# Moving the second mixture's late weight pieces from the first mixture's tile loop to the attention's sampling chunks, in halves by ACT and DVE

## The chip, the cores and the metric

The kernel runs on one core of a Trainium2 chip. The metric is the device time of one execution in microseconds (us); lower is better. Engines are called PE (TensorE), DVE (VectorE), ACT (ScalarE), POOL (GpSimd) and SP (SyncE, which here only issues DMAs).

## The reference, cut to what matters

```python
h = tok_ref(x, weight, bias)                        # 32 sequences of 166 tokens, width 128
h = h + recurrence(layernorm(h))                    # complex linear recurrence, 256 states
h = h + first_mixture(layernorm(h), gate, w1, w2)   # 16 experts of 512, top 2
h = h + sparse_attention(layernorm(h), Wq, Wk, Wv, Wo, idx_sample)
h = h + second_mixture(layernorm(h), w1, b1, w2, b2, router_w, router_b)   # 64 experts of 256, top 42

# first_mixture: sums of silu over an expert's tokens come first, w2 afterwards
h_sum = einsum('tef,te->ef', silu(einsum('td,efd->tef', x, w1)), mask)
y_mean = einsum('ef,edf->ed', h_sum / counts, w2)
out = einsum('tk,tkd->td', routing_w, y_mean[top_idx])

# sparse_attention: every query is scored against 38 sampled keys, the 25 best queries of a head attend in full
QK_sample = einsum('bhld,bhsd->bhls', Q, K[:, :, idx_sample]) * scale
M = QK_sample.max(-1) - QK_sample.mean(-1)
```

## The kernel before

The program is a chain of stages, each a block with one hand-written instruction stream for each engine, tied by semaphores. Every stream is executed in order: a wait at its head holds all that stands behind it. Stages end with a barrier of all engines.

**The expert weights of the second mixture** come in fp32 (8 MB for each of two matrices) and are needed as pairs of fp16 numbers: a rounded value and a correction. They are cut into 32 pieces of 128x1024. Pieces 0 to 15 belong to `ExpertWeights` (L2143) and are split by POOL in four instructions (a cast, a subtraction, a scaling, an addition; `pool_pieces`, L2195). Pieces 16 to 31 belong to `LateWeights` (L2215), which does the same beside the first mixture (`pool_piece`, L2260). The results of all but the first group of experts are stored to DRAM (`expert_factors`) and loaded back by the second mixture.

**The first mixture** (`FirstMixture`, L1273) works on 43 tiles of 384 token slots (`NST`), each of one expert. For each tile SP fetches the slots from DRAM with a transposing DMA into a ring of 8 (L1346). PE forms the 512 hidden features in two sets of 256 (L1403; a set is 4 matmuls of 384 columns into two banks; 4 sets fit), ACT applies silu to a set in place (L1368), DVE sums each feature over the 384 slots (L1374), and then the set is free for PE. So there are 86 sets. SP's stream of this loop (`sync`, L1329) also holds the loads and stores of the late pieces and the four 1 MB loads of the matrix `w2` (`sync_down`, L1325), placed between the transposes by `W2_AT`, `KEEP_FROM` and `KEEP_EVERY`.

**The attention's first stage** (`sparse_attention`, L1502) takes the norm's statistics (its first part), and then works through 16 chunks of two sequences (the sampling part). In chunk `c` PE's stream is, by `work(c, j)`:

```python
samples(c, j, 0); samples(c, j, 1)        # needs ACT's copies kx of chunk c, all four
query(c + 1, 1 - j); key(c + 1, 1 - j)
norm.pe_spread(pe, c + 2, j)              # needs POOL's diagonal of chunk c + 2
for q in range(4):
    token_major(c + 1, 1 - j, q)          # from q = 2 on needs ACT's copy of q - 2
    sampled_scores(c, j, q)
```

PE thus works on the scores of chunk `c` and on the projections of chunk `c + 1` in one pass. ACT's `work(c + 1)` (query and key copies, then three copies for each of four q, L1632 to L1643) goes on at that time, while DVE's `work(c)` takes the maxima of the scores of chunk `c` (L1711, L1713), and before q = 3 normalises chunk `c + 2` (L1269, L1691). ACT is therefore one chunk ahead of DVE. Two banks hold token-major products (4 and 5), and two the scores.

POOL's stream is: diagonals 0 and 1, a piece, diagonal 2, a piece, and so on (L1603 to L1607), so diagonal `c + 2` stands behind the piece that follows diagonal `c + 1`. Before, three pieces are done ahead of diagonal 0. `ExpertWeights` has two raw buffers; SP loads piece `n + 1` before it stores piece `n` (`sync_pieces`, L2185). At the end POOL makes tables for the attention proper (L1608 to L1622).

## Time and profile before

| | |
|---|---|
| median of 3 runs | 2063.67 us (2062.18 to 2066.14) |
| the profiled execution: its own time | 2067.39 us |
| the profiled execution: its span, first to last instruction | 2065.7 us |
| busy: PE, PEld, DVE, ACT, POOL | 1870.1, 1349.7, 1676.4, 1378.0, 1455.0 us |
| granted TensorE clock, mean | 0.939 of full speed |
| first mixture's tile loop | 283.3 to 397.8 us |
| rest of the first mixture | 397.8 to 428.9 us |
| attention: statistics | 428.9 to 455.0 us |
| attention: sampling chunks | 465.9 to 583.2 us |
| attention proper, then the second mixture's set-up | 583.9 to 826 us |
| second mixture, 64 experts | 826 us to the end |

PE is a TensorE matmul, PEld its weight load. "Busy" is the time in which an engine executes; idle time is put down to the instruction that ended it (the releaser). A "granted clock" of 1.00 is 2.4 GHz, one of 0.50 is 1.2 GHz. The rows of the trace stand in a section of their own below.

### The profile page before, as it was taken

The page shows a single profiled execution, that of the slowest core. Times are in us where ns is not written, and L with a number is a line of the kernel's source. Part 1 is how long each engine was busy: PE and PEld are TensorE (multiplying, and loading weights), DVE is VectorE, ACT ScalarE, POOL GpSimd, SP SyncE. Part 2 cuts the span into 40 slices and gives each one's busy share as a digit, 9 for nine tenths or more (in the row PEclk, how much of TensorE's full clock was granted, in tenths as well). Part 3 has the DMA queues.
Part 4 walks back from the last instruction along what each step waited for, and adds up shares of the span by engine and source line. Part 5 has one row for each costly group of instructions (what it writes and reads, how often), then busy time and mean ns, then how long its engine had stood idle before and what let it go on. Part 6 is the DMA issues. An engine that isn't in the chain of part 4 may idle for free.

```text
span 2065.7 us, 50535 instructions
## 1 busy us (share of the span) xinstructions
PE 1870.1 (91%) x17038; PEld 1349.7 (65%) x17038; DVE 1676.4 (81%) x4833; ACT 1378.0 (67%) x2149; POOL 1455.0 (70%) x1098
## 2 busy tenths in 40 slices
PE   7887436789989978999999999999999999999998
PEld 5555213456669855777777777777777777777776
DVE  5887736555678788899999999999999999999998
ACT  4134525424435545888888888888888888888886
POOL 2216679559800032888888888888888888888887
PEclk9998768789989965999999999999999999999999
DMA  3011289523200010000000200000100000000000
GB/s 93 21 35 63 81 246 257 124 67 94 90 1 1 22 63 1 2 2 0 0 0 3 82 2 0 0 0 35 49 1 0 0 0 2 2 10 11 10 11 19
DMA packets 64334, 77.56 MB, mean 38 GB/s; under 512 B 38932, under 2 KB 47028, under 8 KB 62132
## 3 DMA queue, kind: packets, MB, share of 16 engines
q1 hardware_dynamic: 61364, 70.08, 11.7%
q0 software_dynamic: 2816, 5.45, 0.8%
q8 instruction: 94, 1.54, 0.3%
q14 instruction: 60, 0.49, 0.1%
HBM read 42.97 MB, written 24.08 MB: 32 GB/s over the span
## 4 chain that ended last, share of the span: by engine, by line
PE 58%; DVE 3%; issue 2%; ACT 1%; POOL 0%; ACTq 0%; DVEq 0%; POOLq 0%
PE bank L2679 30%; PE bank L2662 28%; DVE m_work L2553 1%; DVE m_best L2550 1%; DVE m_work L2544 0%; PE bank L2632 0%; DVE m_ut L1269 0%; ACT m_h L2485 0%; DVE m_best L2543 0%; DVE m_ex L2555 0%; DVE h L2591 0%; DVE m_red L2556 0%; DVE m_row L2536 0%; POOL m_diag L1255 0%; ACT m_hidden L2482 0%
## 5 line engine op out<-in xcount | busy, mean ns | idle before, releaser
L2679 PEld LDWEIGHTS bank<-weights,m_h 128*128 128x128 f16 x10752 | 649.6, 98 | 194.4 <-DVE hc L2582 82.6
L2430 POOL TENSOR_TENSOR m_h<-m_hidden,m_h 128x896 f16<-128x896 f32 x384 | 725.9, 1890 | 32.0
L2679 PE MATMUL bank<-weights,m_h 128*128 128x128 f16 x10752 | 724.6, 219 | 10.7 <-POOL m_h L2430 2.1
L2582 DVE SCALAR_TENSOR_TENSOR hc<-bank,m_shares,hc 128x128 f32<-128x128 f32 x2688 | 727.2, 342 | 4.3 <-PE bank L2679 4.3
L2482 ACT ACTIVATE m_hidden<-bank,m_b 128x896 f32<-128x896 f32 x384 | 386.9, 1007 | 197.6 <-PE bank L2662 197.5
L2567 DVE TENSOR_TENSOR m_h<-bank,m_h 128x896 f16<-128x896 f32 x384 | 419.2, 1092 | 116.8 <-ACT m_h L2485 116.7
L2428 POOL TENSOR_SCALAR m_h<-m_hidden 128x896 f16<-128x896 f32 x384 | 360.8, 939 | 117.9 <-ACT m_hidden L2482 99.5
L2662 PE MATMUL bank<-m_u_first,weights 128*128 128x448 f16 (+1 forms) x1536 | 417.8, 354 | 5.5 <-DVE h L2591 5.5
L2662 PE MATMUL bank<-m_u_second,weights 128*128 128x448 f16 (+1 forms) x1536 | 417.7, 354 | 0.0
L2479 ACT ACTIVATE bank<-bank,m_b 128x896 f32<-128x896 f32 x384 | 377.6, 983 | 0.6 <-PE bank L2662 0.6
L2485 ACT ACTIVATE m_h<-bank 128x896 f16<-128x896 f32 x384 | 349.1, 909 | 0.0
L2662 PEld LDWEIGHTS bank<-m_u_second,weights 128*128 128x128 f16 x1536 | 150.8, 98 | 141.4 <-issue 2.0
L699 POOL DMA_INDIRECT expert_slots<-weights,ro_slot x88 | 88.9, 1010 | 76.5 <-DVE weights L839 50.6
L1403 PE MATMUL bank<-lru_ut,weights 128*128 128x384 f16 x344 | 74.1, 373 | 74.5 <-DMA lru_ut<-expert_slots 60.0
L1374 DVE TENSOR_REDUCE lru_xc<-bank 128x2 f32<-128x768 f32 x86 | 77.2, 950 | 67.4 <-ACT bank L1368 67.3
L2662 PEld LDWEIGHTS bank<-m_u_first,weights 128*128 128x128 f16 x1536 | 118.2, 98 | 8.1 <-DVE h L2591 6.4
L1368 ACT ACTIVATE bank<-bank 128x768 f32<-128x768 f32 x86 | 64.7, 798 | 82.6 <-PE bank L1403 82.1
L2399 POOL MEMSET m_row<- 128x96 f32 x1 | 0.2, 178 | 157.0 <-POOLq L1827 157.0
L1403 PEld LDWEIGHTS bank<-lru_ut,weights 128*128 x344 | 37.3, 108 | 110.7 <-issue 99.9
L980 POOL TENSOR_TENSOR lru_diag<-ident,rstd 128x332 f32<-128x332 f32 x16 | 13.5, 858 | 65.3 <-PE bank L1147 41.3
L1711 DVE TENSOR_REDUCE at_peak<-bank 83x8 f32<-83x304 f32 x64 | 30.0, 468 | 35.4 <-PE bank L1769 35.2
L1751 PE MATMUL bank<-at_w_qk,at_ut 128*83 128x384 f32 x128 | 52.9, 501 | 0.0
(359 smaller groups left out, 2153.9 us busy)
## 6 DMA issues: line engine op xcount, KB each, us to landing
weights<-expert_factors SPq DMA_DIRECT2D x12, 1024.0 KB, 8.8
lru_w_in<-e_w_dram SPq DMA_DIRECT2D x16, 512.0 KB, 4.5
expert_factors<-lru_w_out SPq DMA_DIRECT2D x16, 512.0 KB, 4.3
ew_raw<-e_w_dram SPq DMA_DIRECT2D x16, 512.0 KB, 3.9
weights<-w_dram SPq DMA_DIRECT2D x16, 256.0 KB, 2.8
weights<-w_dram SPq DMA_DIRECT2D x4, 1024.0 KB, 6.6
expert_factors<-ew_made SPq DMA_DIRECT2D x8, 512.0 KB, 3.0
xs<-x_dram SPq DMA_DIRECT2D x4, 996.0 KB, 11.8
```

The source lines that it names most:

```text
L699: g.indirect_dma_start(out=self.k.slots, out_offset=bass.IndirectOffsetOnAxis(ap=self.slot[0:size, q, n:n + 1], axis=0), in_=self.u_tok[0: ...
L1374: v.tensor_reduce(self.part[:, j // PARTS, j % PARTS * FP:(j % PARTS + 1) * FP], self.set_banks(j), X, ALU.add).then_inc(self.summed, 1)
L1403: last = t.matmul(self.set_banks(n)[:, f % FP], self.w0_parts[m][:, bass.ds(expert * FF0 + f * 128, 128)], self.xt[:, j % RING, m], start= ...
L2428: g.tensor_scalar(h1[:, x, 0], hidden[:, x], 1.0 - SHARE, 1.0, ALU.mult, ALU.mult).then_inc(first_of[1], 1)
L2430: g.tensor_tensor(h1[:, x, 1], hidden[:, x], h1[:, x, 0], ALU.subtract).then_inc(second_of[1], 1)
L2479: sc.activation(banks0(x), banks0(x), ACT.Gelu, bias=b1[:, bass.ds(grp * GE + e, 1), 0]).then_inc(gelu[0], 1)
L2482: sc.activation(two(hidden[:, x % 2]), banks1, ACT.Gelu, bias=b1[:, bass.ds(grp * GE + e, 1), 1]).then_inc(gelu[1], 1)
L2485: sc.activation(two(h0[:, x, 0]), banks0(x), ACT.Copy, scale=1.0 - SHARE).then_inc(first_of[0], 1)
L2567: v.tensor_tensor(two(h0[:, x, 1]), banks0(it), two(h0[:, x, 0]), ALU.subtract).then_inc(second_of[0], 1)
L2582: last = v.scalar_tensor_tensor(acc[:, m * TW:(m + 1) * TW], y[q][:, (n - start) * TW:(n - start + 1) * TW], shares[:, m, e:e + 1], acc[:, ...
L2662: last = t.matmul(bank[:, q], k.weights[:, grp % 2, m, at], uu[:, bass.ds(tb * WB + q * HW, HW)], start=(m == 0), stop=(m == 1))
L2679: last = t.matmul(y[q][:, (n - start) * TW:(n - start + 1) * TW], factors[:, m, n * TW:(n + 1) * TW], k.weights[:, grp % 2, 2 + m, at], st ...
```

## The change

- The late pieces 16 to 31 leave the first mixture. They are cut in halves (128x512, 32 of them), and two halves go with each sampling chunk: ACT rounds a half to fp16 and writes a scaled fp32 copy of it to a buffer `wide`, of which there is one; DVE makes the correction of both in one instruction. ACT's part stands behind q = 1 and q = 3 of its `work(c)`, DVE's behind q = 1 and q = 3 of its own. SP loads and stores the halves.
- The pieces 0 to 15 of POOL are all done beside the sampling chunks; none ahead of diagonal 0. SP's stream for both kinds is one loop over `n`, with the load of piece `n + 1` at the end of round `n`.
- The first mixture's `w2` (4 MB) is loaded into four separate places before the slots' blank ends are written, ahead of the tile loop. The tile loop's SP stream has transposes alone.
- Of the 86 sets, every sixth (14, those with j % 6 == 5) is summed by ACT, with the accumulator output of its silu, in two instructions of 384 columns; DVE sums the other 72.
- The squares of the attention's statistics share memory with the halves' buffers, so SP waits for the last square before it loads a half.

```diff
@@ recurrence, SP
+            mixture.sync_second(sp, y_ready)
             routing.sync_fill(sp)
-            mixture.sync(sp, y_ready)
+            mixture.sync(sp)
@@ FirstMixture
+    def sync_second(self, sp, outputs_made):
         sp.wait_ge(outputs_made, NC)
-        late.sync_load(sp, 0)
-        late.sync_load(sp, 1)
-        sp.wait_ge(k.w0_split, NC)
-        self.sync_down(sp, 0)
+        sp.wait_ge(self.k.w0_split, NC)
+        for q in range(4):
+            self.sync_down(sp, q)
...
-            if j in self.W2_AT:
-                self.sync_down(sp, 1 + self.W2_AT.index(j))
-            if j >= self.KEEP_FROM and (j - self.KEEP_FROM) % self.KEEP_EVERY in (0, 2):
-                late.sync_keep(sp)
...
     def act(self, act):
         for j in range(self.PARTS * NST):
             act.wait_ge(self.up, j + 1)
-            self.nc.scalar.activation(self.set_banks(j), self.set_banks(j), ACT.Silu).then_inc(self.silu, 1)
+            if self.act_sums(j):
+                for f in range(self.FP):
+                    at = j % self.PARTS * self.FP + f
+                    last = self.nc.scalar.activation(self.set_banks(j)[:, f], self.set_banks(j)[:, f], ACT.Silu,
+                                                     accum_out=self.part[:, j // self.PARTS, at:at + 1])
+            else:
+                last = self.nc.scalar.activation(self.set_banks(j), self.set_banks(j), ACT.Silu)
+            last.then_inc(self.silu, 1)
@@ sparse_attention, SP
-                k.expert_weights.sync_pieces(sp, *PIECES_N3)
-                k.expert_weights.sync_pieces(sp, *PIECES_SAMPLE)
+                k.expert_weights.sync_load(sp, 0)
+                k.expert_weights.sync_load(sp, 1)
+                sp.wait_ge(stats.var, NC + DEEP)
+                k.late_weights.sync_load(sp, 0)
+                k.late_weights.sync_load(sp, 1)
+                for n in range(2 * GROUP):
+                    for s in range(2):
+                        k.late_weights.sync_load(sp, 2 * n + 2 + s)
+                        k.late_weights.sync_keep(sp, 2 * n + s)
+                    if n:
+                        k.expert_weights.sync_keep(sp, n - 1)
+                    if 1 <= n < 2 * GROUP - 1:
+                        k.expert_weights.sync_load(sp, n + 1)
@@ sparse_attention, POOL
-                k.expert_weights.pool_pieces(pool, *PIECES_N3)
-                first, end = PIECES_SAMPLE
                 for c in range(NC):
                     norm.pool_diagonal(pool, c, c % 2, stats)
-                    if 1 <= c <= end - first:
-                        k.expert_weights.pool_pieces(pool, first + c - 1, first + c)
+                    if c:
+                        k.expert_weights.pool_pieces(pool, c - 1, c)
+                k.expert_weights.pool_pieces(pool, NC - 1, NC)
@@ sparse_attention, ACT and DVE, behind q = 1 and q = 3
+                        if q % 2:
+                            k.late_weights.act_piece(act, c, q // 2)
...
+                        if q % 2:
+                            k.late_weights.dve_piece(dve, c, q // 2)
@@ LateWeights
     def sync_load(self, sp, i):
         if i >= 2:
             sp.wait_ge(self.raw_read, i - 1)
...
+    def sync_keep(self, sp, i):
         sp.wait_ge(self.split, i + 1)
...
+    def act_piece(self, act, c, s):
+        follows = not isinstance(c, int) or c
+        act.wait_ge(self.raw_in[s], 16 * c + 16)
+        if follows:
+            act.wait_ge(self.kept_out[s], 16 * c)
+        self.nc.scalar.activation(self.made[:, s, 0], self.raw[:, s], ACT.Copy).then_inc(self.rounded, 1)
+        if s or follows:
+            act.wait_ge(self.split, 2 * c + s)
+        self.nc.scalar.activation(self.wide, self.raw[:, s], ACT.Copy, scale=1.0 / SHARE).then_inc(self.raw_read, 1)
+
+    def dve_piece(self, dve, c, s):
+        dve.wait_ge(self.rounded, 2 * c + s + 1)
+        dve.wait_ge(self.raw_read, 2 * c + s + 1)
+        self.nc.vector.scalar_tensor_tensor(self.made[:, s, 1], self.made[:, s, 0], 1.0 - 1.0 / SHARE, self.wide, ALU.mult,
+                                            ALU.add).then_inc(self.split, 1)
```

How the streams stand now is shown at two places. The first is ACT's stream in the sampling part, from q = 1 of a chunk to the next chunk's copies (at_qt and hc are the query and key copies, at_kx the last of the three copies of a q, lw_room the halves' buffers). Before:

```order
L1643 ACTIVATE at_kx<-bank 83x128
L1643 ACTIVATE weights<-bank 83x128 [waits at_token_major_ready]
L1643 ACTIVATE at_v_all<-bank 83x128
L1643 ACTIVATE at_kx<-bank 83x128
L1633 ACTIVATE at_qt<-bank 128x332 [waits at_qt_ready]
L1635 ACTIVATE hc<-bank 128x332 [waits at_kt_ready]
L1643 ACTIVATE weights<-bank 83x128 [waits at_token_major_ready]
```

and with the change:

```order
L1668 ACTIVATE at_kx<-bank 83x128
L2292 ACTIVATE lw_room<-lw_room 128x512 [waits lw_raw_in1]
L2295 ACTIVATE lw_room<-lw_room 128x512 [waits lw_split]
L1658 ACTIVATE at_qt<-bank 128x332 [waits at_qt_ready]
L1660 ACTIVATE hc<-bank 128x332 [waits at_kt_ready]
L1668 ACTIVATE weights<-bank 83x128 [waits at_token_major_ready]
```

Between a chunk's last copy and the next chunk's query copy stand now two instructions, of which the second waits for DVE (`lw_split`).

The second place is SP's stream in the sampling part. Before, loads (L2176) and stores (L2183) of POOL's pieces alternate:

```order
L2176 DMA ew_raw<-e_w_dram 128x1024 x2
L2176 DMA ew_raw<-e_w_dram 128x1024 [waits ew_raw_read] x8
L2183 DMA expert_factors<-ew_made 128x2x1024 [waits ew_split]
L2176 DMA ew_raw<-e_w_dram 128x1024 [waits ew_raw_read]
L2183 DMA expert_factors<-ew_made 128x2x1024 [waits ew_split]
```

With the change (L2210 is the load of a piece of POOL, L2274 and L2281 the load and store of a half; the rows begin with the first two loads):

```order
L2210 DMA ew_raw<-e_w_dram 128x1024 x2
L2274 DMA lw_room<-e_w_dram 128x512 [waits n3_variance]
L2274 DMA lw_room<-e_w_dram 128x512
L2274 DMA lw_room<-e_w_dram 128x512 [waits lw_raw_read]
L2281 DMA expert_factors<-lw_room 128x2x512 [waits lw_split]
L2274 DMA lw_room<-e_w_dram 128x512 [waits lw_raw_read]
L2281 DMA expert_factors<-lw_room 128x2x512 [waits lw_split]
L2274 DMA lw_room<-e_w_dram 128x512 [waits lw_raw_read]
L2281 DMA expert_factors<-lw_room 128x2x512 [waits lw_split]
L2274 DMA lw_room<-e_w_dram 128x512 [waits lw_raw_read]
L2281 DMA expert_factors<-lw_room 128x2x512 [waits lw_split]
L2210 DMA ew_raw<-e_w_dram 128x1024 [waits ew_raw_read]
```

The third load of a POOL piece, piece 2, now stands behind the stores of the halves 0 to 3, and each later one behind two more.

## Rows read from the trace of the kernel before

**Rows 1.** Stretches: us, PE PEld DVE ACT POOL busy, PEclk, DMA share, GB/s.
```profile
283.00:398.00 115.00, 74.30 (x346) 37.51 (x347) 77.16 (x86) 64.69 (x86) 95.96 (x61) 0.84 0.96 237
456.00:466.00 10.00, 10.00 (x26) 5.61 (x26) 5.80 (x10) 2.88 (x12) 9.67 (x8) 0.55 0.18 53
466.00:583.00 117.00, 113.53 (x471) 70.21 (x469) 70.20 (x208) 50.55 (x215) 90.76 (x69) 1.00 0.25 81
744.00:812.00 68.00, 51.03 (x174) 37.45 (x175) 65.53 (x394) 36.47 (x132) 23.79 (x28) 0.50 0.00 1
```

**Rows 2.** Groups by line, the tile loop, 280 to 398 us.
```profile
L1374 DVE TENSOR_REDUCE lru_xc<-bank 128x2 f32<-128x768 f32 x86 | 77.2, 950 | 67.4 <-ACT bank L1368 67.3
L1403 PE MATMUL bank<-lru_ut,weights 128*128 128x384 f16 x344 | 74.1, 373 | 74.5 <-DMA lru_ut<-expert_slots 60.0 <-issue 9.9 <-DVE lru_xc L1374 3.3
L1368 ACT ACTIVATE bank<-bank 128x768 f32<-128x768 f32 x86 | 64.7, 798 | 82.6 <-PE bank L1403 82.1
```

**Rows 3.** SP's queue in order of time, the tile loop's first transposes.
```profile
280.20 5.36 SPq L1346 DMA_TRANSPOSE lru_ut<-expert_slots  x4
```

**Rows 4.** Groups by line, the recurrence stage, 60 to 285 us.
```profile
L1092 DVE SCALAR_TENSOR_TENSOR weights<-weights 128x512 f16<-128x512 f16 x16 | 11.4, 714 | 1.6 <-ACT weights L1008 1.6
L1008 ACT ACTIVATE weights<-weights 128x512 f32<-128x512 f32 x16 | 9.9, 616 | 5.9 <-DVE weights L1092 5.9
L764 ACT ACTIVATION_READ_ACCUMULATOR weights<-weights 128x1 f32 x44 | 8.5, 193 | 0.0
L794 ACT ACTIVATE hc<-bank 16x384 f32<-16x384 f32 x12 | 5.3, 474 | 3.4 <-PE bank L742 3.4
```

**Rows 5.** PE in order of time, sampling stage: start us, us, what.
```profile
465.90 0.54 PE L1760 MATMUL bank<-at_pick,at_kx 83*128 83x39 f32 x4
...
468.42 0.72 PE L1261 MATMUL bank<-at_diag,ones 128*128 128x332 f32 x2
...
470.80 0.69 PE L1769 MATMUL bank<-at_ksm,at_qt 128*83 128x312 f32 x2
...
473.66 0.98 PE L1760 MATMUL bank<-at_pick,at_kx 83*128 83x39 f32 x8
...
583.20 0.36 PE L1460 MATMUL bank<-ident,at_m_all 83*128 83x83 f32 x2 [0.62 <-DVE at_m_all L1713]
```

**Rows 6.** ACT in order of time, sampling stage.
```profile
468.07 0.45 ACT L1633 ACTIVATE at_qt<-bank 128x332 f32<-128x332 f32 x1 [1.36 <-PE bank L1740]
...
469.83 0.27 ACT L1643 ACTIVATE weights<-bank 83x128 f32<-83x128 f32 x1 [0.76 <-PE bank L1751]
...
470.16 0.27 ACT L1643 ACTIVATE at_kx<-bank 83x128 f32<-83x128 f32 x1
```

**Rows 7.** DVE in order of time, sampling stage.
```profile
472.03 0.16 DVE L1713 TENSOR_TENSOR at_m_all<-at_peak,bank 83x8 f32<-83x8 f32 x1
...
473.20 0.16 DVE L1713 TENSOR_TENSOR at_m_all<-at_peak,bank 83x8 f32<-83x8 f32 x1
...
474.75 0.16 DVE L1713 TENSOR_TENSOR at_m_all<-at_peak,bank 83x8 f32<-83x8 f32 x1
```

**Rows 8.** POOL in order of time, sampling stage.
```profile
455.00 1.44 POOL L1255 TENSOR_TENSOR at_diag<-ident,rstd 128x332 f32<-128x332 f32 x2
...
492.57 1.04 POOL L2202 CAST ew_made<-ew_raw 128x1024 f16<-128x1024 f32 x1
...
499.11 0.75 POOL L1255 TENSOR_TENSOR at_diag<-ident,rstd 128x332 f32<-128x332 f32 x1
...
551.14 0.15 POOL L1608 IOTA at_uline<- 83x25 f32 x1
...
555.69 4.14 POOL L1622 TENSOR_SCALAR_AFFINE_SELECT at_expand<-at_expand 128x3200 bf16<-128x3200 bf16 x1
```

**Rows 9.** SP's queue in order of time, sampling stage.
```profile
499.19 0.38 SPq L2183 DMA_DIRECT2D expert_factors<-ew_made  x1
```

**Rows 10.** DMA issues of the page: KB each, us from issue to landing.
```profile
ew_raw<-e_w_dram SPq DMA_DIRECT2D x16, 512.0 KB, 3.9
```

More of the change, by code:

```diff
@@ L992, in _ @@
             mixture.pool_clear(pool)
-            mixture.pool(pool)
         @block.scalar
@@ L1280, with act_sums, dve_sets, wait_summed @@
     FP = FC // PARTS
-    W2_AT = (3, 8, 13)
-    KEEP_FROM, KEEP_EVERY = 4, 5
+    BY_ACT = 6
+    def act_sums(self, n):
+        return n % self.BY_ACT == self.BY_ACT - 1
+    def dve_sets(self, n):
+        return n - n // self.BY_ACT
+    def wait_summed(self, eng, n):
+        if self.act_sums(n):
+            eng.wait_ge(self.silu, n + 1)
+        else:
+            eng.wait_ge(self.summed, self.dve_sets(n + 1))
     def __init__(self, nc, k, routing, w_in, w_out, ut, state_of, xc, xsn):
@@ L1358, in pool_clear @@
         g.memset(self.ym[:], 0.0).then_inc(self.cleared, 1)
-    def pool(self, pool):
-        for i in range(self.late.count):
-            self.late.pool_piece(pool, i)
     def act(self, act):
@@ L1536, in sb1 @@
                 return first.enter_context(nc.sbuf_tensor(f"at_{name}", shape, dt))
+            k.late_weights = LateWeights(nc, k, first)
             norm = Normed(nc, k, first, "at")
-            stats = Statistics(nc, k, first, "n3", CH, HALF, NC, NC // 2)
+            squares = k.late_weights.room[:, 0:DEEP * CH].rearrange("p (n c) -> p n c", n=DEEP)
+            stats = Statistics(nc, k, first, "n3", CH, HALF, NC, NC // 2, squares)
             ut = norm.ut
@@ L1879, in exists, with _ @@
             return not isinstance(b, int) or 0 <= b < B
+        @block.sync
+        def _(sp):
+            k.expert_weights.sync_kept(sp)
         @block.scalar
@@ L2183, in sync_keep, with sync_kept @@
         sp.dma_start(self.k.kept[n // GROUP - 1, :, 2 * mat:2 * mat + 2, cols], self.made[:, n % 2]).then_inc(self.k.kept_out[n % 2], 16)
-    def sync_pieces(self, sp, first, end):
-        self.sync_load(sp, first)
-        for n in range(first, end):
-            if n + 1 < end:
-                self.sync_load(sp, n + 1)
-            self.sync_keep(sp, n)
-        if end == 2 * GROUP:
-            for p in range(2):
-                sp.wait_ge(self.k.kept_out[p], 16 * GROUP // 2)
+    def sync_kept(self, sp):
+        for p in range(2):
+            sp.wait_ge(self.k.kept_out[p], 16 * GROUP // 2)
     def pool_pieces(self, pool, first, end):
@@ L2215, with __init__, sb @@
 class LateWeights:
-    def __init__(self, nc, k, raw, made, left):
+    def __init__(self, nc, k, ctx):
+        def sb(name, shape, dt=F32):
+            return ctx.enter_context(nc.sbuf_tensor(f"lw_{name}", shape, dt))
         self.nc, self.k = nc, k
-        self.raw, self.made, self.left = raw, made, left
+        self.room = sb("room", [128, 5 * HALF_PIECE])
+        self.raw = self.room[:, 0:2 * HALF_PIECE].rearrange("p (j n) -> p j n", j=2)
+        self.wide = self.room[:, 2 * HALF_PIECE:3 * HALF_PIECE]
+        self.made = self.room[:, 3 * HALF_PIECE:].bitcast(F16).rearrange("p (j q n) -> p j q n", j=2, q=2)
         self.raw_in = [k.semaphore(f"lw_raw_in{p}") for p in range(2)]
@@ L2227, in __init__ @@
         self.raw_read = k.semaphore("lw_raw_read")
-        self.widened = k.semaphore("lw_widened")
         self.split = k.semaphore("lw_split")
-        self.first, self.end = PIECES_SENDING
-        self.count = self.end - self.first
-        self.kept = 0
+        self.first, self.end = PIECES_LATE
+        self.count = 2 * (self.end - self.first)
     def sync_load(self, sp, i):
@@ L2236, in sync_load @@
             return
-        n = self.first + i
+        n = self.first + i // 2
         src = self.k.a["e_w1"] if n % GROUP < PIECES else self.k.a["e_w2"]
```

70 lines of the change are left out of this document (27 added, 43 removed).

## The prediction

> **What bounds the kernel now.** I read the table of stretches first, since the two halves of the change lie in two stages with different limits.
>
> In the tile loop of the first mixture (283.3 to 397.8 us) DMA is busy for 0.96 of the time, PE for 74.3 of 115 us, DVE for 77.2 and ACT for 64.7 [rows 1]. The groups by line say who keeps whom waiting: PE's matmuls L1403 stood idle 74.5 us before them, 60.0 of it for the transposed tiles (36.0 of those before the first tile), and DVE and ACT only wait for what comes before them [rows 2]. So the late pieces' loads and stores (7 and 8 MB) and 3 MB of `w2` crowd the tiles, and the loop is bound by DMA, with DVE next.
>
> In the sampling part (465.9 to 583.2 us [rows 5]: 16 chunks, 7.33 us each) PE is busy for 113.5 of 117 us at full clock; DVE for 70.2, ACT for 50.6, POOL for 90.8 [rows 1]. PE bounds it, and nobody makes it wait.
>
> **The tile loop: a gain.** SP's transposes take 5.36 us for four, 1.34 each [rows 3], so 43 x 1.34 = 58 us at least. DVE has 72 sets at most 0.95 us: 68 us [rows 2]. ACT has 72 sets at 0.80 less about 0.06 of overlap, and 14 sets in two instructions of 384 columns, 0.47 each plus 0.19 for reading the accumulator [rows 4]: 53 + 14 x 1.33 = 72 us. PE's 344 matmuls were busy 74 us at a clock of 0.84, in part stretched by waits, so they need less [rows 1, 2]. ACT is the bound; with filling, draining and a first few us at the low clock the loop takes about 77 us instead of 114.5: -37 us. Ends: -42 (ACT never waits), -20 (the transposes alone fill more of the DMA time than I think). The four `w2` loads go ahead of the blank ends and lie beside POOL's indirect sends, which end the wait for the first tile both times: 0.
>
> **The start of the sampling part: a small gain.** Diagonals 0 and 1 came at 455.00 us, behind three pieces of 6.5 us [rows 8]. They now come as soon as the statistics are there, and PE's own last squares set the time: -6 us.
>
> **The sampling part: what is added lies on a ring of waits.** By busy time it would fit. ACT gets 32 halves x 2 x 0.62 = 40 us, DVE 32 x 0.71 = 23 us [rows 4]. But ACT is a chunk ahead of DVE. ACT's second instruction of half (c, 1) waits until DVE has done half (c, 0), for there is one `wide`; DVE does that in its own `work(c)` behind q = 1, whose scores PE makes in pass `c`. ACT's `work(c + 1)` stands behind that wait, and PE in pass `c` needs ACT's copies of chunk `c + 1` for its token-major product q = 2. The same happens at half (c, 0) of the next chunk, whose wait ends behind DVE's q = 3, while PE's samples need ACT's copies of q = 2 and 3.
>
> On top of that SP's stream holds POOL. The load of piece `c` is issued at the end of round `c - 1`, behind the store of half (c - 1, 1), which waits for DVE's last work of pass `c - 1`. POOL's diagonal `c + 2` stands behind piece `c`, and PE in pass `c` needs it for the spread, ahead of all token-major products and scores. So load, piece and diagonal are no longer hidden behind PE; they follow the end of the pass before.
>
> One turn, from DVE's end of half (c - 1, 1) to its end of half (c, 1), at full clock:
>
> 1. SP: a store's issue 0.4 [rows 9], the load's landing 3.9 [rows 10], and its passing on 0.2: 4.5.
> 2. POOL: the piece 6.54 (492.57 to 499.11), the diagonal 0.75 [rows 8], 0.2 to pass on: 7.5. Sum 12.0.
> 3. PE: from the spread to the start of the scores of q = 1, 468.42 to 470.80: 2.4 [rows 5]. Sum 14.4.
> 4. DVE: from there to the end of the measure of q = 1, 472.19: 1.4 [rows 5, 7]; half (c, 0) 0.71 [rows 4]. Sum 16.5.
> 5. ACT: the scaled copy 0.62 [rows 4]; query and key copies and three copies of q = 0: 468.07 to 470.43 less the wait of 0.76: 1.6 [rows 6]; 0.4 to pass on. Sum 19.1.
> 6. PE, then DVE: token-major and scores of q = 2, to the end of its measure: about 2.1 (0.65 for the product, then as in 4) [rows 5, 7]. Sum 21.2.
> 7. DVE: normalising chunk c + 2 and q = 3, from 473.36 to 474.91: 1.6 [rows 7]; half (c, 1) 0.7. Sum 23.5.
>
> PE works about 7.3 of these 23.5 us. The clock does not stay up in such a stage: between 744 and 812 us PE is busy for 51.0 of 68 us, with waits of a microsecond or two between bursts, and is granted 0.50 throughout; in 456 to 466 us it is 0.55, after the wait for POOL [rows 1]. At 1.2 GHz the four PE steps on the ring (3, the latency in 4, 6 twice) take about 4 us more: 27.5 us. This is the value I take, as both rows lie nearer to a PE that waits most of the time than the full clock of a packed stage does.
>
> The Trainium skill (TensorE: Matmul & The Clock Gate, HAM oscillation) describes loops in which each tile's matmuls are shorter than the wait ahead of them, so that every tile starts at the half clock. By that rule a turn is the 27.5 us; by the 1.00 of the sampling row alone it would be 23.5, and the forecast below 2251.
>
> The turns: chunk 0 takes about 14 us (its two halves' waits, no late load: pieces 0 and 1 are loaded early). Chunk 1 has the ring of ACT and DVE alone: 0.8 for ACT's scaled copy, 1.2 for its copies of q = 2 and 3, 2.1 for PE from samples to spread (473.66 less 468.42 taken from 7.33 [rows 5]), then steps 3 to 7 (11.5): 15.6, or 21.6 at half clock; I take 20. Chunks 2 to 13 have the full turn: 12 x 27.5 = 330, plus 0.4 for a store of POOL's pieces in four of them, 332. Chunk 14 needs no spread: 20. Chunk 15 has no next chunk: 9. Sum 395 against 117.3: **+278 us**. Behind it, piece 15 is loaded at the end of chunk 14 and followed by POOL's tables, 551.14 to 559.83 [rows 8]: 0.8 + 4.1 + 6.5 + 8.7 = 20 us, of which chunk 15 covers 9: +11 us at the barrier.
>
> **Sum:** 2067.4 (the profiled execution's own time) - 37 - 6 + 278 + 11 = 2313. That execution stands 3.7 us above the median of the three runs, so **2310 us** is forecast. Everything behind the barrier is unchanged and only shifted.
>
> **The rivals.**
>
> *Hidden after all (on the other side).* The ring would not bind if ACT's and DVE's halves fitted into their idle time with PE still packed. For it: ACT would be busy for 90 and DVE for 93 of 117 us, both below PE. Against it: the order of the streams. It would decide if ACT's waits for `lw_split` were met on arrival, that is if DVE's part of a chunk came in the same pass as ACT's. Then the gains alone are left, 2063.7 - 43 = 2021 us. Chance 0.04. The Trainium skill (Perfetto Trace Analysis, Identifying the Most-Contended Engine) goes by occupancy for ACT and DVE, and by that rule PE would go on setting the pace and this case would be the result.
>
> *The ring of ACT and DVE alone.* If POOL's loads came in time, turns would be 15.6 to 21.6 us: 14 + 14 x (15.6 to 21.6) + 9 = 241 to 325, so +124 to +208 with no tail: 2144 to 2229, middle 2190 us. Against it: SP's stream as the order shows it. Chance 0.08.
>
> *The tile loop gains nothing* (the transposes bind by themselves): 2310 + 37 = 2347 us. Against it: four transposes were issued in 5.36 us. Chance 0.04.
>
> *All of it, at full clock:* chunk 0 13, chunk 1 15.6, 12 x 23.5 + 2, then 15 and 8.5: 336, so +219 instead of +278: 2251 us. This is a bound of the forecast, not a case of its own.
>
> **How the numbers follow.** The forecast's case has 0.81, its neighbours at 2190 and 2347 have 0.12, the hidden case 0.04, and 0.03 is left for a gain and a loss that meet. The range goes from 2225 (below the full clock's 2251, for a larger gain in the tile loop and faster hand-overs, and into the rival ring at half clock) to 2350 (1 us more in each turn, 12, half the gain of the loop, 18, and the third rival). A difference under 0.2% (4 us) is what a measurement of this kernel cannot tell from none. Faster 0.04, same 0.01, slower 0.95.
>
> **What the changed profile would show.** The tile loop lasts 72 to 80 us, ACT has the least idle time in it, and PE no longer waits for the transposes after the first. The sampling part lasts 370 to 420 us, its turns 26 to 29; the spread L1261 waits for POOL's diagonal about 12 us less the passage to it; ACT's L2295 waits for DVE L2300 twice a turn; POOL's cast L2230 waits for the DMA; PEclk is near 0.5. The forecast would be wrong if the diagonal is there when PE wants it, or if ACT's scaled copies never wait.

## The result and the profile after

The changed kernel took a median of 2293.10 us (2287.57 to 2293.56, 4 runs) against 2063.27 us (2062.18 to 2066.14) for the kernel before: a ratio of 1.1105, 95% interval 1.1085 to 1.1126. The profiled execution took 2293.09 us, its span is 2291.4 us, 225.7 us longer than before, and the mean granted clock is 0.887.

Where the time lies, by landmarks of both traces (us; the landmarks are the first matmul of the tile loop, PE's first transpose behind the loop, PE's first spread L1261, the attention proper's first product with `att_oh` (L2040 before, L2073 after), and the first row of the second mixture's softmax):

| stretch | before | after | difference | forecast |
|---|---|---|---|---|
| up to the tile loop | 283.3 | 284.7 | +1.4 | 0 |
| tile loop | 114.5 | 84.5 | -30.0 | -37 |
| to the first spread | 58.1 | 47.8 | -10.3 | -6 |
| to the attention proper | 130.2 | 406.8 | +276.6 | +289 |
| attention proper | 157.3 | 158.0 | +0.7 | 0 |
| second mixture to the end | 1322.3 | 1309.6 | -12.7 | 0 |
| sum | 2065.7 | 2291.4 | +225.7 | +246 |

The table of stretches after (columns as in [rows 1]):

```profile
284.00:370.00 86.00, 69.48 (x348) 35.66 (x348) 64.60 (x73) 66.68 (x128) 0.00 (x0) 0.90 0.50 97
416.00:800.00 384.00, 207.37 (x494) 110.29 (x493) 94.28 (x238) 79.52 (x282) 103.88 (x73) 0.63 0.21 66
800.00:822.00 22.00, 5.46 (x18) 2.79 (x18) 6.09 (x16) 3.24 (x12) 15.48 (x13) 0.63 0.38 131
```

In the sampling part (416 to 800 us) no engine is busy for more than 54%, and the granted clock is 0.63, where [rows 1] have a full PE at 1.00. Over the one turn that is shown below (480.19 to 507.54) it is 0.56. In the tile loop DMA fell from 0.96 to 0.50, and from 237 to 97 GB/s.

The groups by line in the tile loop after, which answer to [rows 2]:

```profile
L1413 PE MATMUL bank<-lru_ut,weights 128*128 128x384 f16 x344 | 68.8, 349 | 48.0 <-DMA lru_ut<-expert_slots 34.5 <-issue 9.9 <-DVE lru_xc L1384 0.4
L1384 DVE TENSOR_REDUCE lru_xc<-bank 128x2 f32<-128x768 f32 x72 | 64.5, 951 | 48.5 <-ACT bank L1375 48.4
L1375 ACT ACTIVATE bank<-bank 128x768 f32<-128x768 f32 x72 | 54.3, 799 | 48.5 <-PE bank L1413 48.1
...
L1372 ACT ACTIVATE bank<-bank 128x384 f32<-128x384 f32 x28 | 13.5, 490 | 0.5 <-PE bank L1413 0.5
L1372 ACT ACTIVATION_READ_ACCUMULATOR bank<-bank 128x1 f32 x28 | 5.7, 204 | 0.0
```

PE waits for the transposes 34.5 us, all of them before the first tile. What is left is "issue 9.9", which stood in [rows 2] too and which I had passed over. In order of time it is two stops:

```profile
317.87 7.27 PE L1413 MATMUL bank<-lru_ut,weights 128*128 128x384 f16 x32 [5.69 <-issue]
...
348.52 9.13 PE L1413 MATMUL bank<-lru_ut,weights 128*128 128x384 f16 x40 [4.19 <-issue]
```

These are the places where PE loads the owners of the next tiles into its registers (`load_rows`, 16 ahead of tile 16 and 11 ahead of tile 32).

The waits of the sampling part, 400 to 800 us (engine line, what it waited for, us in total, times, longest):

```profile
ACT lw_room L2295 <- DVE lw_room L2300: 287.6, 30, 17.4
...
POOL ew_made L2230 <- DMA ew_raw<-e_w_dram: 139.9, 7, 21.0
POOL weights L2230 <- DMA ew_raw<-e_w_dram: 130.2, 6, 31.7
PE bank L1261 <- POOL at_diag L1255: 88.4, 12, 8.5
```

One turn of the ring in order of time (start us, us, what, idle time ahead of it and its releaser), from one load of a piece (L2210) to the next:

```profile
482.29 0.47 SPq L2210 DMA_DIRECT2D ew_raw<-e_w_dram  x1
...
486.61 1.04 POOL L2230 CAST weights<-ew_raw 128x1024 f16<-128x1024 f32 x1 [18.22 <-DMA ew_raw<-e_w_dram]
...
493.14 0.74 POOL L1255 TENSOR_TENSOR at_diag<-ident,rstd 128x332 f32<-128x332 f32 x1
...
493.93 1.48 PE L1261 MATMUL bank<-at_diag,ones 128*128 128x332 f32 x2 [6.96 <-POOL at_diag L1255]
...
498.73 0.69 PE L1798 MATMUL bank<-at_ksm,at_qt 128*83 128x312 f32 x2
...
500.25 0.69 DVE L2300 SCALAR_TENSOR_TENSOR lw_room<-lw_room 128x512 f16<-128x512 f16 x1
...
500.98 0.63 ACT L2295 ACTIVATE lw_room<-lw_room 128x512 f32<-128x512 f32 x1 [16.04 <-DVE lw_room L2300]
...
502.82 1.57 PE L1780 MATMUL bank<-at_w_qk,at_ut 128*83 128x384 f32 x2 [3.39 <-ACT at_kx L1668]
...
504.18 1.25 PE L1798 MATMUL bank<-at_ksm,at_qt 128*83 128x312 f32 x2
...
506.46 0.50 DVE L1269 TENSOR_TENSOR at_ut<-hc,bank 128x332 f32<-128x332 f32 x1 [0.22 <-issue]
...
508.51 0.69 DVE L2300 SCALAR_TENSOR_TENSOR lw_room<-lw_room 128x512 f16<-128x512 f16 x1
...
509.64 0.47 SPq L2210 DMA_DIRECT2D ew_raw<-e_w_dram  x1
```

The step from SP to POOL takes 486.61 - 482.29 = 4.3 us (forecast 4.5), POOL's piece and diagonal to PE's spread 7.3 (7.5), PE to the scores of q = 1 4.8 (2.4 at full clock), DVE to the end of its half 2.2 (2.1), ACT until PE goes on 1.9 (2.6), PE and DVE for q = 2 to DVE's normalising 3.6 (2.1), DVE to its half of q = 3 done 2.7 (2.3), and 0.4 for the store's issue. These make 27.3 us.

### The profile page after: what moved, and what is told of

The parts are those of the page before. It is cut to its first block, busy times and chain, and to the rows that moved or that the text cites. A ratio compares the mean times of both kernels' runs of the same rounds, so it can differ in the third digit from the quotient of the medians.

```text
span 2291.4 us, 50696 instructions
## 1 busy us (share of the span) xinstructions
PE 1947.5 (85%) x17038; PEld 1375.1 (60%) x17038; DVE 1682.2 (73%) x4851; ACT 1408.5 (61%) x2255; POOL 1355.0 (59%) x1034
## 4 chain that ended last, share of the span: by engine, by line
PE 52%; DVE 3%; issue 2%; ACT 1%; POOL 1%; ACTq 0%; DVEq 0%; POOLq 0%
PE bank L2706 27%; PE bank L2689 25%; DVE m_work L2580 1%; DVE m_best L2577 0%; DVE m_work L2571 0%; PE bank L2659 0%; DVE m_ut L1269 0%; POOL m_h L2457 0%; ACT m_h L2512 0%; DVE m_best L2570 0%; DVE m_ex L2582 0%; DVE h L2618 0%; ACT m_hidden L2509 0%; DVE m_red L2583 0%; DVE m_row L2563 0%
## 5 line engine op out<-in xcount | busy, mean ns | idle before, releaser
L2706 PEld LDWEIGHTS bank<-weights,m_h 128*128 128x128 f16 x10752 | 641.0, 98 | 190.1 <-DVE hc L2609 75.7
L2295 ACT ACTIVATE lw_room<-lw_room 128x512 f32<-128x512 f32 x32 | 20.1, 629 | 291.9 <-DVE lw_room L2300 291.9
L1780 PE MATMUL bank<-at_w_qk,at_ut 128*83 128x384 f32 x128 | 82.9, 747 | 50.2 <-ACT at_kx L1668 50.2
L1413 PE MATMUL bank<-lru_ut,weights 128*128 128x384 f16 x344 | 68.8, 349 | 48.0 <-DMA lru_ut<-expert_slots 34.5
L1384 DVE TENSOR_REDUCE lru_xc<-bank 128x2 f32<-128x768 f32 x72 | 64.5, 951 | 48.5 <-ACT bank L1375 48.4
L2230 POOL CAST ew_made<-ew_raw 128x1024 f16<-128x1024 f32 x8 | 8.3, 1037 | 151.6 <-DMA ew_raw<-e_w_dram 151.6
L1261 PE MATMUL bank<-at_diag,ones 128*128 128x332 f32 x32 | 22.1, 800 | 88.4 <-POOL at_diag L1255 88.4
L2230 POOL CAST weights<-ew_raw 128x1024 f16<-128x1024 f32 x8 | 8.3, 1038 | 130.2 <-DMA ew_raw<-e_w_dram 130.2
```

Of the source, the lines that this page charges most:

```text
L1413: last = t.matmul(self.set_banks(n)[:, f % FP], self.w0_parts[m][:, bass.ds(expert * FF0 + f * 128, 128)], self.xt[:, j % RING, m], start= ...
L1780: t.matmul(k.bank[0:HALF, 4 + q % 2, 0:384], ut[:, j, q * HALF:(q + 1) * HALF], w_qk[:].rearrange("p a b -> p (a b)"), start=True, stop=Tr ...
L2706: last = t.matmul(y[q][:, (n - start) * TW:(n - start + 1) * TW], factors[:, m, n * TW:(n + 1) * TW], k.weights[:, grp % 2, 2 + m, at], st ...
```

## The experiments

**1. The load of POOL's piece at the start of a round.** It is meant to take POOL off the ring, and the hand-over of `wide` between ACT and DVE stays.

```diff
                 for n in range(2 * GROUP):
+                    if 1 <= n < 2 * GROUP - 1:
+                        k.expert_weights.sync_load(sp, n + 1)
                     for s in range(2):
                         ...
                     if n:
                         k.expert_weights.sync_keep(sp, n - 1)
-                    if 1 <= n < 2 * GROUP - 1:
-                        k.expert_weights.sync_load(sp, n + 1)
```

> SyncE issues the load of POOL's next piece at the start of each round, ahead of the two waits for the halves; nothing else differs from the changed kernel. Theory (the turn of 27 us is one ring: SyncE's load of ew_raw, POOL's 7.5 us of pieces and diagonals, PE, VectorE and ScalarE's hand-over of `wide`, back to SyncE): POOL and 4.2 us of landing leave the ring, and what stays is ScalarE and VectorE handing `wide` to one another across chunks, 15.6 to 21.6 us a turn; the sampling part falls from about 395 us to 240 to 325 us, POOL's 11 us behind the last chunk go too, total 2130 to 2215 us. Rival 1 (the added work itself, ScalarE's and VectorE's halves and DMA traffic, makes the turn): unchanged within 10 us, 2283 to 2303. Rival 2 (only PE's low granted clock): unchanged too, with the granted clock of 400 to 800 us still at 0.64.

Measured: 2213.92 us (2209.42 to 2219.89), ratio 1.0725 [1.0699, 1.0750]. That is 79 us less than the changed kernel, so both rivals are out, but it stands at the upper edge of what I expected. POOL's casts in order of time tell why:

```profile
531.16 1.04 POOL L2230 CAST weights<-ew_raw 128x1024 f16<-128x1024 f32 x1 [8.91 <-DMA ew_raw<-e_w_dram]
...
550.80 1.04 POOL L2230 CAST ew_made<-ew_raw 128x1024 f16<-128x1024 f32 x1 [11.91 <-DMA ew_raw<-e_w_dram]
...
605.75 1.04 POOL L2230 CAST ew_made<-ew_raw 128x1024 f16<-128x1024 f32 x1 [27.95 <-DMA expert_factors<-ew_made]
```

The first seven turns take 16.7 us each (414.1 to 531.2), as expected, and PE waits for no diagonal in them; the seven from piece 8 on take 25.0 (550.8 to 725.7). From there POOL's pieces are stored too, and a cast waits for the store of the piece two before, which SP issues behind the halves of another round. The store was a second member of the ring, hidden behind the load in the changed kernel.

**2. ACT's half one chunk later.** ACT does the half of chunk c - 1 in `work(c)` (and the last two behind the loop), so that it is level with DVE.

```diff
-                        if q % 2:
-                            k.late_weights.act_piece(act, c, q // 2)
+                        if q % 2 and exists(c - 1):
+                            k.late_weights.act_piece(act, c - 1, q // 2)
```

> ScalarE does its half of the last chunk's piece in this chunk's work, so that it and VectorE alternate on `wide` without either being a chunk ahead; the load of POOL's pieces stays late. Theory (one ring with both parts in it): the wait of ScalarE on VectorE for `wide` (288 us, 30 times, in the changed kernel) goes nearly altogether, the ring keeps SyncE's late load and POOL's 7.5 us, the turn falls from 27.3 to 19.5 us (full clock) to 24 us (half clock): 14 turns less by 3.3 to 7.8 us, total 2184 to 2247 us. Rival 1 (added work makes the turn): 2283 to 2303. Rival 2 (POOL's late load alone decides, ScalarE's wait is only slack): the turn stays over 26 us, total over 2270.

Measured: 2218.62 us (2216.82 to 2222.07), ratio 1.0749 [1.0731, 1.0767], in the middle of the theory's range. ACT's wait for DVE's half is gone from the waits; the turn is 20.7 us (413.2 to 558.1 for seven), then 22.0. PE now waits for POOL at nearly every spread:

```profile
PE bank L1261 <- POOL at_diag L1255: 150.4, 12, 13.4
POOL ew_made L2232 <- DMA ew_raw<-e_w_dram: 117.7, 8, 16.6
POOL weights L2232 <- DMA ew_raw<-e_w_dram: 94.1, 6, 18.9
```

Taking out either wait alone thus gives 74 to 79 us of the 277 (in experiment 1 with the stores' ring still in the way).

**3. Both edits,** of 1 and of 2.

> Both edits. Theory: neither ring is left, a chunk costs what it did before the change, 7.3 to 8 us a turn, with PE mostly at the full granted clock between 440 and 560 us; with the gain of about 30 us in the tile loop and the 8 us at the start of sampling that the changed kernel shows, total 2020 to 2035 us, faster than both kernels. Rival 1 (the halves cost ScalarE and VectorE 1.6 and 1.8 us twice a chunk beside work that PE waits for, so the turn is 10 to 12 us): total 2060 to 2095. Rival 2 (the engines' added work is the bound, as in the changed kernel): over 2200.

Measured: 2127.12 us (2121.95 to 2128.48), ratio 1.0297 [1.0278, 1.0317]. A miss for the theory and for both rivals: 166 us less than the changed kernel, but 92 to 107 more than the theory wanted. Seven turns take 11.5 us, the seven after them 18.8, and what POOL waits for is named:

```profile
POOL ew_made L2232 <- DMA expert_factors<-ew_made: 79.5, 6, 15.4
PE bank L1261 <- POOL at_diag L1255: 65.9, 8, 11.7
...
POOL weights L2232 <- DMA ew_raw<-e_w_dram: 28.2, 6, 11.5
```

A ring of two chunks was left. The load of piece n + 1 is issued behind the halves of chunk n - 1, and 4.1 + 7.3 us later the diagonal lets PE into pass n + 1: two passes for one trip. From piece 8 on the store, behind the halves of one chunk more, closes a shorter one.

**4. The same, with all sums by DVE.**

```diff
     def act_sums(self, n):
-        return n % self.BY_ACT == self.BY_ACT - 1
+        return False
     def dve_sets(self, n):
-        return n - n // self.BY_ACT
+        return n
```

> As the kernel with both edits, but VectorE alone forms the sums of all 86 sets of tiles, as before the change. Theory (in the changed tile loop VectorE's sums, the two stops of PE for register loads and ScalarE's share the time): VectorE is busy 86 x 0.89 = 77 us of some 85, so the loop gets 0 to 8 us longer than with a sixth on ScalarE, total 0 to 8 us over the kernel with both edits. Rival (the sixth on ScalarE is what gained the loop its 30 us): 20 us or more over it.

Measured: 2132.25 us (2127.34 to 2134.66), 5.1 over the kernel with ACT's sixth, as the theory had it. The loop lasts 89.8 us (280.90 to 370.69), not 84.6 (282.08 to 366.65). So of the 30 us gained in the loop some 5 are the sums', and the rest comes with what left it, the late pieces and `w2`.

**5. Store and load of POOL's pieces ahead of the halves,** on top of both edits.

```diff
                 for n in range(2 * GROUP):
-                    if 1 <= n < 2 * GROUP - 1:
-                        k.expert_weights.sync_load(sp, n + 1)
+                    if n:
+                        k.expert_weights.sync_keep(sp, n - 1)
+                    if n < 2 * GROUP - 2:
+                        k.expert_weights.sync_load(sp, n + 2)
                     for s in range(2):
                         ...
-                    if n:
-                        k.expert_weights.sync_keep(sp, n - 1)
```

> As the kernel with both edits, but at the start of round n SyncE now stores POOL's piece n - 1 and loads piece n + 2, before it waits for any half. That kernel's turns were 11.5 us for the first seven and 18.8 us after, when POOL's pieces are also stored; POOL waited there 28 + 8 us for the load and 80 us for the store of the piece two before. Theory (what is left is the same kind of ring, only two chunks long: load or store behind the halves of an earlier chunk, then 4.2 + 7.3 us to the diagonal): with load and store a round earlier both waits go, turns of 7.5 to 9 us, the sampling part 120 to 150 us, total 2035 to 2065 us. Rival (ScalarE's and VectorE's halves themselves, 2 x 1.25 and 2 x 0.7 us a chunk, break PE's pace and its clock): turns stay at 11 us or more, total over 2080.

Measured: 2050.34 us (2049.16 to 2054.18), ratio 0.9918 [0.9896, 0.9940]. The order of SP's stream alone is worth 77 us here, and the kernel is now 0.8% faster than the kernel before. The total fell into the forecast's range, but the turns (7.5 to 9 us) did so only at first: PE's spreads stand 8.2 us apart in the mean from 426.16 to 499.54, and 11.9 from there to 547.12, where POOL's pieces wait for their stores again. From the first spread to the attention proper it takes 172.1 us, 41.9 more than in the kernel before.

**6. The halves' loads and stores on ACT's queue,** on top of edit 2. SP's stream is POOL's pieces alone, behind the first two halves. The run differs in two more things: each load of a POOL piece is issued at the start of a round, as in edit 1, and ACT's chunks are written out and no longer a loop.

```diff
     def act_piece(self, act, c, s):
         ...
         if s or follows:
-            act.wait_ge(self.split, 2 * c + s)
+            self.sync_keep(act, 2 * c + s - 1)
         self.nc.scalar.activation(self.wide, ...).then_inc(self.raw_read, 1)
+        self.sync_load(act, 2 * c + s + 2)
```

> ScalarE's half aligned with VectorE's, and ScalarE issues the loads and stores of the halves on its own queue, where it has made or met every condition they wait for; SyncE's stream is POOL's pieces alone, each load a piece ahead. ScalarE's chunks are written out, not looped. Theory: no ring is left; turns of 7.5 to 9 us as with the stores and loads early on SyncE's queue, total 2035 to 2070 us, a few us worse than that one for 4 issues of 0.35 us a chunk on ScalarE. Rival (the halves' work itself): total over 2080.

Measured: 2039.21 us (2035.77 to 2043.85), ratio 0.9859 [0.9799, 0.9918]. The range held; that it would be worse than experiment 5 did not: it is 11 us better. POOL now casts every 7.8 us (412.6 to 529.4 for fifteen) and waits for no load and no store. How much of the 11 us the written-out chunks give was not tried.

**7 and 8. PE's register loads ahead of the tile loop,** on top of 5 and of 6.

```diff
+        experts = []
+        for first in range(0, NST, 16):
+            experts += load_rows(self.nc, pe, routing.owner_i[0:1, first:min(first + 16, NST)], 0, E0 - 1)
         for j in range(NST):
-            if j % 16 == 0:
-                experts = load_rows(self.nc, pe, routing.owner_i[0:1, j:min(j + 16, NST)], 0, E0 - 1)
-            expert = experts[j % 16]
+            expert = experts[j]
```

> As the kernel with early loads and stores on SyncE's queue, and PE reads all 43 owners of the tiles (three loads of registers) ahead of the tile loop, where it waits 34 us for the first tile anyway. Theory (the two stops of 5.7 and 4.2 us are the 7 us by which the loop came out longer than I forecast): 8 to 10 us less than the kernel without this edit. Rival (ScalarE bounds the loop and the four free sets cover such a stop): 0 to 2 us less.

> The kernel with the halves on ScalarE's queue plus PE's register loads ahead of the tile loop: 8 to 10 us less than without them by my theory, 0 to 2 by the rival; beside the other pair this measures the same edit a second time.

Measured: 2040.97 us (2038.56 to 2041.53) and **2029.80 us** (2025.06 to 2030.43), each 9.4 less than the kernel without the edit. The second has a ratio of 0.9801 [0.9743, 0.9858] to the kernel before. Its tile loop lasts from 284.2 to 356.2, 72 us, which is 12.6 less than in kernel 6 (281.44 to 366.01). Between 284 and 356 us the granted clock is 0.96, not 0.91. By the landmarks of the table above its span is 37.2 us shorter than that of the kernel before (2028.5 and 2065.7). The loop gives 42.5 of them, the way to the first spread 9.0, and the second mixture 15.7, by a cause that stays open (below). From the first spread to the attention proper it still takes 158.8 us, 28.6 more than the 130.2 before.

**9. Pieces 0 and 1 ahead of diagonal 0,** on top of 8.

```diff
+                k.expert_weights.pool_pieces(pool, 0, 2)
                 for c in range(NC):
                     norm.pool_diagonal(pool, c, c % 2, stats)
-                    if c:
-                        k.expert_weights.pool_pieces(pool, c - 1, c)
-                k.expert_weights.pool_pieces(pool, NC - 1, NC)
+                    if 1 <= c < NC - 1:
+                        k.expert_weights.pool_pieces(pool, c + 1, c + 2)
```

> The kernel with the halves on ScalarE's queue and early register loads, and POOL does its pieces 0 and 1 ahead of diagonal 0, in the 14 us in which it waits there for VectorE's variances; the loop then ends two turns earlier for POOL. Theory (POOL paces the sampling part: cast after cast stands 7.98 us apart without idle time on it): the first diagonal stays within 1 us, the last two turns run at PE's 7.3 us and POOL's tables end 16 us earlier: 1 to 6 us less than without this edit. Rival (PE's chunks end last in any case and POOL's pace does not matter): within 1 us of it. Other side (piece 1 takes longer beside VectorE's statistics and delays the first diagonal): 1 to 4 us more.

Measured: 2032.96 us (2029.87 to 2035.30), 3 more than kernel 8, the other side. Piece 0's load had not landed when POOL came to it, so diagonals 0 and 1 came 4 us later, and piece 2's load stands in SP's stream behind the wait for the last square:

```profile
392.68 1.04 POOL L2232 CAST weights<-ew_raw 128x1024 f16<-128x1024 f32 x1 [5.30 <-DMA ew_raw<-e_w_dram]
...
405.90 1.43 POOL L1255 TENSOR_TENSOR at_diag<-ident,rstd 128x332 f32<-128x332 f32 x2
419.38 1.04 POOL L2232 CAST weights<-ew_raw 128x1024 f16<-128x1024 f32 x1 [12.04 <-DMA ew_raw<-e_w_dram]
```

**10. Without DVE's part of the halves,** on top of 8. DVE's instruction is left out, and ACT writes a plain copy in the correction's place, so the stored corrections are not the right ones.

```diff
-        self.nc.scalar.activation(self.wide, self.raw[:, s], ACT.Copy, scale=1.0 / SHARE).then_inc(self.raw_read, 1)
+        act.wait_ge(self.rounded, 2 * c + s + 1)
+        self.nc.scalar.activation(self.made[:, s, 1], self.raw[:, s], ACT.Copy).then_inc(self.split, 1)
```

> The kernel with the halves on ScalarE's queue and early register loads, but VectorE's instruction of the halves is left out: ScalarE's second one writes the correction's place in fp16 itself (the values of the second groups' corrections are then not the reference's). ScalarE's and DMA's work stay as they are. Theory (VectorE's instruction with two operands in SBUF and POOL's subtraction and addition, also with two, shut each other out: POOL's go from 2.12 to 2.44 to 2.56 us and VectorE's from 0.69 to as much as 3.6): POOL's return to 2.12 us, the turn from 7.98 to 7.3 us, 8 to 15 us less in all. Rival (DMA traffic of 206 GB/s or ScalarE's work slows POOL): POOL's stay at 2.4 to 2.5 us and the time within 3 us.

Measured: 2014.94 us (2012.97 to 2017.29), 14.9 less than kernel 8. POOL's subtractions and additions (line, duration min/median/max in ns, first and last start), in kernel 8:

```profile
L2236 POOL TENSOR_TENSOR ew_left<-ew_raw,ew_made x8: 2126/2555/2566, 465.8 to 521.4; 128x1024 f32<-128x1024 f32 x8
L2240 POOL TENSOR_TENSOR ew_made<-ew_left,ew_made x8: 2127/2438/2445, 469.6 to 524.7; 128x1024 f16<-128x1024 f32 x8
```

and without DVE's part:

```profile
L2234 POOL TENSOR_TENSOR ew_left<-ew_raw,ew_made x8: 2126/2129/2133, 462.9 to 512.8; 128x1024 f32<-128x1024 f32 x8
L2238 POOL TENSOR_TENSOR ew_made<-ew_left,ew_made x8: 2121/2123/2131, 466.3 to 516.2; 128x1024 f16<-128x1024 f32 x8
```

The theory holds: 2.56 and 2.44 us go back to 2.13 and 2.12, although ACT's and DMA's work stayed. PE's turn, from spread to spread, fell from 8.6 us in the mean of thirteen (416.92 to 528.45; an undisturbed one is 8.0, the longest 11.2) to 7.6 (417.65 to 516.57), which is 12.6 of the 14.9 us.

**11. The register loads ahead, in the kernel before** (the edit of 7 and 8 alone).

> The kernel before, with PE's register loads ahead of its tile loop and nothing else. Theory (that loop was bound by DMA, busy for 0.96 of it, so that PE's two stops of 10 us in all lay beside transfers that were late anyway): 0 to 3 us less, where the same edit gave 9.4 us in both kernels in which the DMAs had left the loop. Rival (the stops are serial there too): 8 to 10 us less.

Measured: 2064.26 us (2062.61 to 2066.13, 10 runs) against 2063.60, ratio 1.0002 [0.9992, 1.0011]: nothing, as the theory had it. The row of PE's matmuls there shows where the 9.9 us of [rows 2] went:

```profile
L1404 PE MATMUL bank<-lru_ut,weights 128*128 128x384 f16 x344 | 75.1, 381 | 72.0 <-DMA lru_ut<-expert_slots 68.3 <-DVE lru_xc L1374 3.4
```

The stops are gone, and PE waits for the transposes 68.3 us, not 60.0. The same stops were free while DMA bounded the loop and cost 9.4 us once it did not.

**12. POOL's tables ahead of diagonal 0,** on top of 8 (the table instructions are moved, nothing else).

> The kernel with the halves on ScalarE's queue and early register loads, and POOL makes the tables for the attention proper (8.7 us) in the 14 us in which it waits for the variances, ahead of diagonal 0, not behind its last piece. Theory (they are free there, and behind the last piece the last fill of 4.1 us holds up a VectorE half for 3.6 us in the last chunks, and with it PE): the first diagonal unmoved, 2 to 6 us less than without this edit (2029.8). Rival (the last chunks wait for something else): within 2 us of it. Other side (the tables delay VectorE's statistics and the first diagonal): 1 to 5 us more.

Measured: 2027.60 us (2024.50 to 2028.75), ratio 0.9811 [0.9795, 0.9828]. That is 2.2 less than kernel 8, too little to be told from it by these runs; the stretch from diagonal 0 to the attention proper, which the edit touches, is 4.7 us shorter (155.2 for 159.9, to the first product L2065).

## Why the prediction held, and where it did not

The forecast was 2310 us with a range from 2225 to 2350, and 2293 came. The mechanism was the forecast's, and its sizes were near. The terms were off to both sides: the tile loop by 7 us to the one, the start of sampling, the sampling part and the second mixture by 4, 12 and 13 to the other. In sum the change was 20 us less than forecast (225.7 for 246), so errors of both signs met in the total, which is luck, and the change behind the barrier was not foreseen at all.

- **The tile loop** was mis-sized: -30.0, not -37. "ACT is the bound" was wrong for this kernel. ACT was busy for 66.7 us of the loop's 84.5 by the stretches (its groups by line add to 73.5, but overlap). The 7 us over my 77 are PE's two stops, 9.9 us in all. With them ahead of the loop it took 72 us in kernel 8, with PE, ACT and DVE busy for 65.9, 66.2 and 64.0 of them, and ACT waited for PE for 2.5 us behind the first tile, where it had waited for 14.2 in the changed kernel. So ACT came near to being the bound, but only with the stops gone. I had the number in [rows 2] and gave it no step. In the kernel before, it cost nothing (experiment 11). It was free only by a cover that the change took away.
- **The start of the sampling part** was -10.3, not -6. PE had waited 4.96 us for POOL's diagonals, and this is gone (POOL now stood ready 14.3 us before the variances came); that is the forecast's term, 5.0 for 6. The rest was not in the forecast: 2.0 us come from the stretch before the statistics (31.3 to 29.2, granted clock 0.85 and 0.94), and 3.3 from the statistics themselves, where POOL's pieces had held up DVE's short instructions and, through ACT, PE's squares. Beside the pieces DVE was busy for 15.6 us in this stage, without them for 10.5. Here is one such instruction, which ends with POOL's; after the change the same instruction (L1705, at 413.97) takes 0.26 us:

```profile
446.36 2.16 POOL L2210 TENSOR_TENSOR weights<-ew_left,weights 128x1024 f16<-128x1024 f32 x1
...
447.12 1.42 DVE L1678 TENSOR_SCALAR at_pick<-at_pos 83x2 f32<-83x2 f32 x1
```
- **The sampling part** was the ring that I described: late load, POOL, PE, DVE, ACT, DVE. Chunk 0 took 11.6 us (14), chunk 1 17.0 (20), chunks 2 to 13 324.8, which is 27.1 each (332 with 27.5 each), chunk 14 18.9 (20). Piece 15 and the tables set the end, at 821.6 us. In all 276.6 for 289. Experiments 1, 2, 3 and 5 take the ring apart: without the late load 79 us less, without ACT's wait for DVE 74 less, without both 166, and with the store and load early 243.
- **The clock.** The step "at 1.2 GHz the four PE steps on the ring" was right: the two parts of the turn with most of PE's work took 4.8 and 3.6 us for 2.4 and 2.1 at full clock, 3.9 more where I had 4. In the turn shown, the spread behind POOL's diagonal took 1.48 us for two (0.72 at full clock, [rows 5]), and of the products behind it only the scores of q = 1 took the full clock's 0.69. "PEclk is near 0.5" holds for that turn (0.56). The 0.63 of the whole part comes from its first chunks (0.77 up to 480 us) and from its later turns (0.58 to 0.67 from 617 us on). The Trainium skill (TensorE: Matmul & The Clock Gate, HAM oscillation) has each burst that is shorter than the wait ahead of it start at the half clock; the trace agrees, with 1.44 to 1.48 for 0.72 at every spread that waited for POOL. The burst behind ACT's copies, 5.6 us behind a wait of 3.39, started there too (1.57 for 0.81). In kernels 5 and 6, with PE packed, the clock is 0.96 and 0.98 between 440 and 520 us, so it follows from the ring.
- **Behind the barrier** I had "everything is unchanged and only shifted". The second mixture took 12.7 us less. Its rate between two equal stretches (columns as in [rows 1]), before:

```profile
1000.00:1300.00 300.00, 298.00 (x3397) 216.93 (x3395) 273.56 (x755) 253.03 (x284) 267.01 (x189) 1.00 0.04 15
```

and after:

```profile
1238.00:1538.00 300.00, 300.00 (x3441) 217.63 (x3440) 276.92 (x764) 256.85 (x287) 270.12 (x193) 1.00 0.04 15
```

3441 matmuls, not 3397, in 300 us. From the first row of its softmax to the end it lasts 1306.6 to 1310.9 us in the changed kernel and in the eleven made from it, and 1322.3 and 1321.5 in the kernel before and the one made from that (11). PE's 10752 matmuls L2679 there are as long as before, 219 ns, but PE's idle time ahead of them fell from 10.7 to 3.5 us, which is part of it. So it comes with the change and not with a run, but none of the experiments undid what brings it: its cause stays open.

Of the rivals, "the ring of ACT and DVE alone" (turns of 15.6 to 21.6 us, 2144 to 2229) is what the first seven turns of experiment 1 show (16.7 us). Its total, 2214, holds the stores' ring as well, which made the later turns 25.0. "Hidden after all" (2021) came true in no kernel: 8 and 12 come near its time (2030 and 2028), but the sampling part still takes 28.6 us more than before in kernel 8, made up for by the register loads and by the second mixture. For the changed kernel the Trainium skill's rule (Perfetto Trace Analysis, Identifying the Most-Contended Engine), which takes the engine with the highest occupancy as the bottleneck and judges TensorE by its weight loads and not by its matmuls, names none that is near its limit: of 384 us the weight loads are busy for 110, POOL for 104, DVE for 94 and ACT for 80. The trace decides here by its waits.

## What to carry to other kernels

Work that fits into an engine's idle time is only free if every wait it brings is met on arrival in all streams that it is put into, the DMA queue's too: a load behind a store in SP's stream made POOL wait, and through POOL PE. Walk the ring of waits in order of time from one load to the next, and look how many passes it spans; an engine with a piece of the work should be level with its partner, and each kind of transfer belongs on a queue whose other waits are its own. With all these waits met, the moved work was still not free: beside DVE's part of it POOL's pieces took longer. A stop that costs nothing beside a bound must get a price when the change takes that bound away.

## What was not expected of the hardware

- DVE's correction of a half, two SBUF operands, and POOL's instructions shut each other out. In kernel 8, two instructions that overlapped:

```profile
531.70 4.14 POOL L1645 TENSOR_SCALAR_AFFINE_SELECT at_expand<-at_expand 128x3200 bf16<-128x3200 bf16 x1
...
532.75 3.59 DVE L2303 SCALAR_TENSOR_TENSOR lw_room<-lw_room 128x512 f16<-128x512 f16 x1 [0.55 <-ACT lw_room L2297]
```

DVE's instruction takes 0.69 us alone and lasted here to 0.5 us behind the end of POOL's, and POOL's tensor operations took 2.44 to 2.56 us beside it, for 2.13 [rows 8, where a piece took 6.54]. It is no idle time of the two engines in any view; only their durations show it. DVE's part of the halves, this included, costs kernel 8 14.9 us (experiment 10). The Trainium skill (SBUF — State Buffer, Who interferes with whom) says that a VectorE instruction with two SBUF inputs contends with a GpSimd one that reads SBUF, for a pair of ports that only one of them holds at a time; the trace agrees. In the kernel before, POOL's pieces held up short DVE instructions of the statistics in the same way (1.42 us for 0.26, above).
- The loads of 16 and of 11 values into PE's registers stopped it for 5.7 and 4.2 us.
- Four issues a chunk of 0.35 to 0.44 us on ACT's queue cost less than the same four in SP's stream: kernel 6 is 11 us faster than kernel 5, though ACT's written-out chunks have a share in it that was not measured. In experiment 5 POOL still waited 24.5 us for its stores, in 6 not at all, which fits.
